# Folding the one-hot products of a graph kernel in two operations each, with the steps of a running maximum dealt out singly

## The reference

```python
h = jnp.maximum(_layernorm(x, axis=-1), 0.0)
x_i, x_j = h[dst], h[src]
msg = jnp.concatenate([x_i, x_j - x_i], axis=-1) @ W.T + b
out = jax.ops.segment_max(msg, dst, num_segments=x.shape[0])
x = x + jnp.where(jnp.isfinite(out), out, 0.0)
```

## Time and profile before

| | |
|---|---|
| median of 3 runs | 862.87 us |
| profiled execution, first to last instruction (span) | 862.0 us |
| what lies around the span (difference) | 0.8 us |
| DVE busy | 790.4 us, 92%, 1283 instructions |
| POOL busy | 619.0 us, 72%, 631 instructions |
| PE busy | 544.8 us, 63%, 2442 instructions |
| ACT busy | 422.6 us, 49% |
| chain that ended last, by engine | DVE 41%, POOL 19%, issue 19%, DMA 11%, PE 7% |
| granted TensorE clock, mean | 0.866 of full speed |

### The profile page before, as it was taken

How to read it: one execution, slowest core, us unless ns; L and a number is a source line. 1 busy time by engine, 2 the same in 40 slices (tenths; PEclk the granted TensorE clock), 3 DMA queues, 4 the chain that set the end, 5 groups by cost and what they waited for, 6 DMA issues and landing times.

```text
span 862.0 us, 8032 instructions
## 1 busy us (share of the span) xinstructions
PE 544.8 (63%) x2442; PEld 263.8 (31%) x2442; DVE 790.4 (92%) x1283; ACT 422.6 (49%) x279; POOL 619.0 (72%) x631
## 2 busy tenths in 40 slices
PE   1565898000000677787766857788888888888871
PEld 1553466000000223232222323233333333333341
DVE  7989999989999899989989899899999998898897
ACT  3785314060147077656577569655565655742000
POOL 1577267788777777677777776777767777777774
PEclk9799899555555799988989988999999999999995
DMA  8951003232374766455655556556555666444347
GB/s 253 218 153 25 10 15 95 69 83 68 96 210 99 237 165 197 134 176 141 184 155 169 155 139 184 157 182 191 173 174 177 193 180 221 159 118 138 76 96 212
DMA packets 114693, 126.74 MB, mean 147 GB/s; under 512 B 19542, under 2 KB 96836, under 8 KB 114379
## 3 DMA queue, kind: packets, MB, share of 16 engines
q1 hardware_dynamic: 95090, 86.33, 33.0%
q0 software_dynamic: 19376, 38.94, 18.2%
q10 hardware_dynamic: 184, 0.96, 0.3%
HBM read 86.43 MB, written 40.57 MB: 147 GB/s over the span
## 4 chain that ended last, share of the span: by engine, by line
DVE 41%; POOL 19%; issue 19%; DMA 11%; PE 7%; ACT 1%; POOLq 0%; DVEq 0%; SPq 0%
POOL rows L746 14%; DMA rows<-near_table,idx 8%; DVE maxima L1278 8%; DVE acc L1334 8%; PE ps L869 7%; POOL hT L725 3%; DVE ohs L1240 3%; DVE sorts_mem L1068 2%; DVE sorts_mem L1067 2%; DVE hT L1287 2%; DVE ohs L1231 2%; POOL ohs L719 2%; DVE ohs L1229 1%; DVE rows L1240 1%; DMA ohs<-in_dst,begin_i 1%
## 5 line engine op out<-in xcount | busy, mean ns | idle before, releaser
L746 POOL DMA_INDIRECT rows<-near_table,idx x503 | 516.1, 1026 | 181.2 <-issue 132.8
L869 PE MATMUL ps<-ohs,near 128*128 128x481 fp8e3 x1404 | 319.0, 381 | 82.9 <-DVE acc L1334 76.3
L1334 DVE TENSOR_TENSOR acc<-ps,acc 128x1924 f32<-128x1924 f32 x196 | 343.5, 1779 | 29.3 <-PE ps L869 29.0
L607 ACT ACTIVATE ohs<-ohs,spike 128x6272 fp8e3<-128x6272 uint8 x36 | 197.9, 5513 | 72.0 <-DMA ohs<-winners 72.0
L869 PEld LDWEIGHTS ps<-ohs,near 128*128 128x128 bf16 x1404 | 134.3, 100 | 267.7 <-DVE acc L1334 90.2
L1278 DVE SCALAR_TENSOR_TENSOR maxima<-maxima,fresh,rows 128x128 f32<-128x128 f32 x503 | 176.8, 351 | 17.3 <-DMA rows<-near_table,idx 3.6
L602 ACT ACTIVATE hT<-k,off 128x1600 bf16<-128x1600 int16 (+6 forms) x49 | 65.9, 1392 | 154.8 <-DVE hT L1292 154.8
L869 PE MATMUL ps<-sorts_mem,near 128*128 128x481 fp8e3 x507 | 116.3, 385 | 28.1 <-DVE acc L1334 25.4
L607 ACT ACTIVATE sorts_mem<-sorts_mem,spike 128x6272 fp8e3<-128x6272 uint8 x13 | 71.7, 5515 | 35.9 <-DMA sorts_mem<-winners 35.9
L857 PE MATMUL ps<-flags,ones 128*128 128x11 f32 x2 | 0.6, 362 | 138.5 <-DVE spare L1312 138.5
L869 PEld LDWEIGHTS ps<-sorts_mem,near 128*128 128x128 bf16 x507 | 49.2, 101 | 94.9 <-DVE acc L1334 31.0
(11 more groups left out here) (192 smaller groups left out, 472.6 us busy)
## 6 DMA issues: line engine op xcount, KB each, us to landing
running_max<-maxima SPq DMA_DIRECT2D x63, 512.0 KB, 3.6
ohs<-winners SPq DMA_DIRECT2D x36, 784.0 KB, 6.1
sorts_mem<-winners SPq DMA_DIRECT2D x13, 784.0 KB, 6.2
rows<-near_table,idx POOLq DMA_INDIRECT x503, 3.1
acc<-in_x SPq DMA_DIRECT2D x6, 512.0 KB, 8.0
near_table<-acc SPq DMA_DIRECT2D x12, 256.0 KB
base<-in_x SPq DMA_DIRECT2D x1, 2744.0 KB
out_x<-hT SPq DMA_DIRECT2D x12, 224.0 KB
```

Source lines behind the costliest of these rows:

```text
L607: nc.scalar.activation(oh[t % OHS], oh_bytes[t % OHS], ACT.Abs_reciprocal_sqrt, bias=spike[:, 0:1], scale=float(SPIKE), saturate=False).th ...
L746: nc.gpsimd.indirect_dma_start(rows[:, n % (SLOTS * GATHERS), :], None, near_table[:, :], bass.IndirectOffsetOnAxis(idx[:, n:n + 1], 0)).t ...
L869: last = nc.tensor.matmul(bank(4 * (n % 2) + c - UNITS[r][0])[:, 0:CHUNK], near[:, t, part, :], oh[t % OHS][:, at:at + CHUNK], start=part ...
L1334: V.tensor_tensor(into, found[:, 0:z - a, 0:CHUNK], into, ALU.max).then_inc(max_done, 1)
```

## The change

Each fold becomes two operations: a unit of 4 chunks is folded as 2 and 2 chunks, one of 3 chunks as 2 and 1 (`FOLDS`). A tile has 8 folds in place of 4 rounds, 196 operations more in all. The semaphore `max_done` counts both, so PE, which waits for a whole unit, waits for twice the number.

The plan has new numbers: a chain step costs 0.26 us, a second one behind it 0.38 us (0.355 us each before); data count as there 1.0 us after the modelled landing (1.5 us before); behind a piece ahead of the folds stand at most two chain steps, behind a fold or a tree's piece after the "disorder" piece at most one (four before). The four operations of the second list's selection become four pieces, with the waits between them as before.

```diff
-LANDING, MARGIN, MOST_STEPS = 4.6, 1.5, 4
+LANDING, MARGIN = 4.6, 1.0
+STEP, NEXT_STEP = 0.26, 0.38
 UNITS = ((0, 4), (4, 7), (7, 10), (10, 13))
+FOLDS = ((0, 2), (2, 4)), ((0, 2), (2, 3)), ((0, 2), (2, 3)), ((0, 2), (2, 3))
...
-    pieces = [("lists", 11.0, 2.2), ("check", 1.1, 1.5), ...
+    pieces = [("lists", cost, 2.0) for cost in (2.5, 3.9, 1.4, 2.4)] + [("check", 1.1, 1.5), ...
...
-        for r in range(4):
-            pieces += [("round", (2.15, 1.65, 1.65, 1.65)[r], 1.26)]
+        pieces += [("fold", 0.11 + 0.495 * (z - a), 1.26) for folds in FOLDS for a, z in folds]
...
     for name, cost, gather in pieces:
         now += cost
+        dense += name == "disorder"
...
-        while n < total and len(here) < MOST_STEPS:
+        while n < total and len(here) < (1 if dense else 2):
...
-            now += 0.355
+            now += NEXT_STEP if here else STEP
...
-                if name == "round":
-                    rounds_done += 1
-                    t = rounds_done // rounds + AHEAD
-                    if rounds_done % rounds == rounds - 1 and t < tiles:
+                if name == "fold":
+                    folds_done += 1
+                    t = folds_done // (2 * rounds) + AHEAD
+                    if folds_done % (2 * rounds) == 2 * rounds - 2 and t < tiles:
                         load(t)
...
                     if n >= 2:
-                        pe.wait_ge(max_done, n - 1)
+                        pe.wait_ge(max_done, 2 * (n - 1))
...
-            def dense_round(n):
-                r = n % rounds
-                a, z = UNITS[r]
-                found = ps[:, 4 * (n % 2) * 512:4 * (n % 2 + 1) * 512].rearrange("p (c w) -> p c w", w=512)
-                dve.wait_ge(dense_made, n + 1)
-                into = acc[:, a * CHUNK:z * CHUNK].rearrange("p (c w) -> p c w", w=CHUNK)
+            def dense_fold(n, i):
+                u, v = FOLDS[n % rounds][i]
+                a = UNITS[n % rounds][0]
+                found = ps[:, (4 * (n % 2) + u) * 512:(4 * (n % 2) + v) * 512].rearrange("p (c w) -> p c w", w=512)
+                into = acc[:, (a + u) * CHUNK:(a + v) * CHUNK].rearrange("p (c w) -> p c w", w=CHUNK)
+                if i == 0:
+                    dve.wait_ge(dense_made, n + 1)
...
                 if n >= rounds:
-                    dve.wait_ge(max_done, n - rounds + 1)
-                V.tensor_tensor(into, found[:, 0:z - a, 0:CHUNK], into, ALU.max).then_inc(max_done, 1)
+                    dve.wait_ge(max_done, 2 * (n - rounds) + i + 1)
+                V.tensor_tensor(into, found[:, :, 0:CHUNK], into, ALU.max).then_inc(max_done, 1)
```

More of the change, by code:

```diff
@@ L102, in schedule @@
 def schedule():
-    pieces = [("lists", 11.0, 2.2), ("check", 1.1, 1.5), ("check", 1.9, 1.5), ("check", 1.9, 1.5)]
+    pieces = [("lists", cost, 2.0) for cost in (2.5, 3.9, 1.4, 2.4)] + [("check", 1.1, 1.5), ("check", 1.9, 1.5), ("check", 1.9, 1.5)]
     pieces += [("sort", 1.42, 1.5)] * 21 + [("tiles", 2.3, 1.7)]
@@ L128, in schedule @@
     now, issue, n, landed, done, listed, steps = 0.0, 0.0, 0, [], [], None, []
+    dense = 0
     for name, cost, gather in pieces:
         now += cost
+        dense += name == "disorder"
         if name == "list":
@@ L473, in maxima_store @@
                              maxima[:, i % 2, :, :]).then_inc(maxima_out[i % 2], 16)
-            trees_begun, left_of_tree, rounds_done = 0, 0, 0
+            trees_begun, left_of_tree, folds_done = 0, 0, 0
             for k, name in enumerate(names):
@@ L757, in _ @@
                     with pool.If(pool.value_load(disorder[0:1, 0:1], min_val=0, max_val=1 << 23) > 0):
-                        pool.wait_ge(max_done, rounds * tiles)
+                        pool.wait_ge(max_done, 2 * rounds * tiles)
                         for at, g in finals_at.items():
@@ L875, in _ @@
             pe.wait_ge(decided, 1)
-            pe.wait_ge(max_done, rounds * tiles)
+            pe.wait_ge(max_done, 2 * rounds * tiles)
             for g, (a, z) in enumerate(spans):
@@ L1029, in lists @@
                                      deg[:, None, a:q].to_broadcast([P, KS, q - a]), ALU.is_ge))
+                yield
                 settled()
@@ L1032, in lists @@
                                             L[:, a:z, :].rearrange("p j k -> p k j"), ALU.mult, ALU.max))
+                yield
                 settled()
                 then(V.tensor_tensor(S1[:, :, a:z], S0[:, :, a:z], nid[:, None, a:z].to_broadcast([P, KS, z - a]), ALU.is_equal))
+                yield
                 settled()
                 then(V.scalar_tensor_tensor(S0[:, :, a:z], S1[:, :, a:z], float(IS_SELF), S0[:, :, a:z], ALU.mult, ALU.add))
-                settled()
+                yield
             def merges():
@@ L1332, in dense_round @@
                 if n >= rounds:
-                    dve.wait_ge(max_done, n - rounds + 1)
-                V.tensor_tensor(into, found[:, 0:z - a, 0:CHUNK], into, ALU.max).then_inc(max_done, 1)
-            lists(0)
+                    dve.wait_ge(max_done, 2 * (n - rounds) + i + 1)
+                V.tensor_tensor(into, found[:, :, 0:CHUNK], into, ALU.max).then_inc(max_done, 1)
+            for _ in lists(0):
+                pass
             for i in range(len(steps_of_sort)):
@@ L1344, in _ @@
             loser_list(0)
-            checks, flagging, wording, moving = check(), loser_flags(1), second_words(), compact(1)
-            wordings, sorts, trees_begun, left_of_tree, dense_rounds = 0, 0, 0, 0, 0
+            listing, checks, flagging, wording, moving = lists(1), check(), loser_flags(1), second_words(), compact(1)
+            wordings, sorts, trees_begun, left_of_tree, folds_done = 0, 0, 0, 0, 0
             for k, name in enumerate(names):
                 if name == "lists":
-                    lists(1)
+                    next(listing)
                 if name == "check":
@@ L1379, in _ @@
                     left_of_tree -= 1
-                if name == "round":
-                    dense_round(dense_rounds)
-                    dense_rounds += 1
+                if name == "fold":
+                    dense_fold(folds_done // 2, folds_done % 2)
+                    folds_done += 1
                 for n in served[k]:
```

## The result

The changed kernel takes **868.11 us** in the median of 8 runs (866.38 to 871.58); the kernel before, run beside it, 863.23 us (8 runs, 862.81 to 866.01). The ratio is 1.0056 with a 95% interval from 1.0041 to 1.0072: it is slower by about 0.6%. The forecast was no change at 862.8 us. The time lies inside the range of 855 to 870 us, but the forecast case is wrong.

A forecast was written before the change was run, and what follows sets the result against it. The prediction took POOL's list of transfers to bound the kernel, with DVE's 27.5 us off the path. It summed 862.0 + 0 - 1.1 + 1.0 + 0 = 861.9 us, with 0.8 around the span 862.8; range 855 to 870 us.

The forecast's parts named there:

- the forecast case: Whole kernel: no change, within 0.2% or 1.7 us of the time before; chance 0.36.
- The bound: POOL's list of 552 transfers is the path from 113.4 to 853.2 us; DVE only has to stay close behind.
- rival B: DVE is the limit after all, so its 27.5 us arrive: 835 us; chance 0.04.
- DVE's sum: DVE up to the last fold: 13.7 - 38.1 - 3.1 = -27.5 us, last fold from 834.8 to about 807 us.
- The stores at the end, -1.1: SP's last two stores start 1.1 us earlier, as nine groups are joined earlier; from 0 to -1.5 us.
- Longer gathers beside single steps, +1.0: POOL's gathers beside chain steps that begin apart get longer, +1.0 us in all; bounds nothing to 47 us.
- fall between gathers: The joins moved ahead on DVE were said to fall between POOL's gathers; no cost was put on them.
- rival D: Single steps hold up POOL's gathers, one in ten longer by 0.12 us, 4.7 us: 866 us; chance 0.08.
- The waits for landing, 0: POOL's 8.6 us of waits for landings stay the same in sum, 0; bounds -8.6 to +39 us.
- rival C: Loads fall badly and lock: 13 pairs of batches lose 1.2 us each, 15.6 in place of 8.6: 870 us; chance 0.21.
- The pairs ahead of the folds: On DVE ahead of the folds, 26 groups become 52 pairs: 36.9 us becomes 33.8.

The follow-up runs named there:

- e12: The changed kernel with three batches in flight and at most two chain steps behind every piece in place of one: 868.12 us, 1.0062.
- e9: The kernel before (whole folds) with new costs and margin, at most two steps behind every piece, three batches in flight: 849.19 us, 0.9848.
- e11: The changed kernel with three batches in flight and all thirteen joins behind the last chain step: 856.13 us, 0.9927.
- e1: The changed kernel, but POOL waits for the landing of the batch three ahead instead of two: 857.15 us, 0.9921.
- e3: The changed kernel, but from tile 8 on only the first half of each tile's one-hot bytes is loaded: 860.79 us, 0.9964.
- e5: The changed kernel with split folds, but the plan's old numbers and up to four chain steps behind a piece: 883.97 us, 1.0246.
- e4: The kernel before with at most two steps behind a piece ahead of the folds and the new step costs: 862.24 us, 0.9984.
- e2: The kernel before, but POOL waits for the landing of the batch three ahead instead of two: 859.71 us, 0.9951.
- e8: The kernel before with pairs ahead of the folds and the wait for the batch three ahead: 860.96 us, 0.9975.

## Why the prediction was wrong

**The bound: right.** POOL's list was the path before and stayed it. DVE's last fold moved by 27 us and nothing of it arrived; rival B is out.

**DVE's sum: right, by terms that partly offset each other.** Added up over the stretch from the first to the last fold, DVE's own time in folds grows by 14.9 us (13.7 predicted). The steps there, with the waits ahead of them, fall by 41.7 (38.1 predicted). The waits of folds for PE grow by 7.0 us; the sum had nothing for them, but the text named up to 10. The rest are 3.3 us less for the trees and a first fold that comes 4.3 us earlier (3.1 predicted). The folds by form after, answering:

```profile
L1341 DVE TENSOR_TENSOR acc<-ps,acc 128x962 f32<-128x962 f32 x245 | 281.7, 1156 | 38.1 <-PE ps L872 37.8
L1341 DVE TENSOR_TENSOR acc<-ps,acc 128x481 f32<-128x481 f32 x147 | 96.2, 654 | 0.0
```

From start to start of the next operation they are 1.070 and 0.568 us in the median, so an extra operation costs 0.07 us, as the prediction worked out. The Trainium skill ("Perfetto Trace Analysis", Optimizing Scalar/DVE Operations) gives about 125 ns of access for a DVE operation on PSUM; these rows show 0.07 us from start to start, and the rows decide. The 24 us by which the last folds of e12 and e9 differ are not a dearer operation either: 13.4 us are fold operations, 196 of 0.07 us, and 7.8 us waits for PE.

**The stores at the end, -1.1: wrong.** SP's last store did come right behind the last join, at 859.55 us. But the trace has a last instruction of POOL, a drain, that ends after all stores, in both kernels. Source L197 before, then L200 after (duration in ns, start in us):

```profile
L197 POOLq DRAIN  x1: 14416/14416/14416, 847.4 to 847.4; - x1
```

```profile
L200 POOLq DRAIN  x1: 16001/16001/16001, 848.9 to 848.9; - x1
```

It ends at 861.8 and 864.9 us, 9.6 and 9.5 us after the last final started (852.22 before; after, 855.38):

```profile
855.38 0.94 POOL L728 DMA_INDIRECT hT<-running_max,end_row  x1 [0.30 <-issue]
```

Stores that end before the drain are worth nothing. In the kernel before, too, SP was through at 861.2 us, 0.6 us ahead of the drain's end, so earlier stores had nothing to win there.

**Longer gathers beside single steps, +1.0: the step that failed.** It measured +4.4 us, and most of that is not beside the steps. The table sorts the issues of POOL (gathers and finals) from 285 us on by what DVE runs 0.1 to 0.5 us after an issue's start; a tree or a join goes ahead of a chain step where both run. The entries are rounded.

| us above 0.945, all issues | before | after | difference |
|---|---|---|---|
| an operation of a tree | 7.4 | 9.4 | +2.0 |
| the second operation of a join | 0.7 | 2.3 | +1.6 |
| a chain step, none of these | 1.5 | 2.7 | +1.2 |
| folds, the first operation of a join, or nothing | 0.0 | -0.3 | -0.3 |

So the chain steps cost 1.2 us, about the size that the prediction gave them, and the operations of trees and joins, which it put at nothing, cost 3.6. The mean of 0.951 us was taken from 560 to 620 us, where no trees stand, and laid over all 390 gathers as 2.3 us. In the stretch with trees the kernel before already had 6.7 us (its 0.986 above), and the change added most there. The joins were said to "fall between gathers"; e11, in which they stand behind the last step, shows that they do not (2.2 us fall to 0.4). A gather that starts with a tree's operation, in e1, on DVE and on POOL:

```profile
413.31 0.98 DVE L1293 TENSOR_TENSOR hT<-hT 128x1600 bf16<-128x1600 bf16 x1
```

```profile
413.32 1.79 POOL L749 DMA_INDIRECT rows<-near_table,idx  x1 [0.30 <-issue]
```

It is 0.84 us longer. The longest of the changed kernel starts beside a chain step that a tree's operation follows 0.18 us later, and is 1.15 us longer (POOL, then DVE):

```profile
474.25 2.09 POOL L749 DMA_INDIRECT rows<-near_table,idx  x1 [0.30 <-issue]
```

```profile
474.43 1.10 DVE L1293 TENSOR_TENSOR hT<-hT 128x1800 bf16<-128x1800 bf16 x1
```

The first row of the table, over all traces, goes with single steps behind the pieces of the trees: 9.4 to 11.7 us in the four kernels that have them (the changed kernel, e1, e3, e11), 4.1 to 7.4 us in the ten others, e5 with its split folds among them. That single steps among the trees make the gathers meet the trees so often is a reading of these traces; why they do stays open. The rule of rival D is that of the Trainium skill ("SBUF — State Buffer", Who interferes with whom): a DVE instruction with two SBUF inputs contends with a GpSimd instruction that reads SBUF. The rows agree with it: a tree's operation and the second of a join have two inputs in SBUF, too, while beside folds, which have one, no issue of the fourteen traces from 285 us on is more than 0.02 us longer. The prediction's price was for the chain steps alone. Rival D's 4.7 us thus came nearly out, but not by its mechanism.

**The waits for landing, 0: wrong by 3.1 us.** The lock of rival C appeared, over seven pairs of batches rather than thirteen and at 0.2 to 0.8 us rather than 1.2. That the waits are for landings is shown by e1, in which all are gone, and that most of them hang on the loads by e3.

**What the sum lacked.** The pairs ahead of the folds were counted on DVE alone; on POOL they are worth 3.9 us, 3.6 of them from 113 to 200 us, as in e4. With the first gather's 0.7 us that is the gain of 4.6 us ahead of the folds; without it the 4.4 us of longer issues and the 3.1 us of waits would have shown in full, and the time would be near 868.1 + 4.6 = 872.7 us, an estimate. So it is luck that the time lies inside the range.

## What to carry to other kernels

Where the bound is an engine that issues transfers, do not stop at showing that another engine's gain is off its path: add up what its own instructions have over their least duration, stage by stage, since a denser order elsewhere can make them longer. Take such a mean from the stage that has the disturbing operation, not from a clean one. When waits name an engine, compare when that engine freed the resource with when the wait ended; here one more batch in flight, with pairs and whole folds, was worth 14.2 us, and 27 us less on DVE alone were worth nothing.

## What was not expected of the hardware

- In all fourteen traces POOL's drain ends 9.5 to 9.6 us after the start of the last indirect transfer. In nine of them it sets the end of the span; in the other five (e2, e4, e5, e8, e12) SP's last stores are later.
- The issue of an indirect transfer takes 0.945 us on POOL, but from 285 us on up to 1.15 us more in the changed kernel when a DVE operation with two SBUF inputs runs near its start.
- Chain steps in pairs in place of fours beside the sort cut what POOL's issues have above 0.945 us, from 113 to 200 us, from 25.2 to 21.6 us.
